# Moving the second batch's front of an attention kernel behind the first score tiles

## Chip, cores, metric

The kernel runs on one core of a Trainium2 chip. The metric is the device time of one execution in microseconds (us). Before the change three runs gave 232.41, 233.00 and 233.81 us, a median of 233.0 us.

## What is computed

Two batches of 512 tokens with 128 features pass through four parts: a gated layer whose weights are picked per batch (`argmax` of `cond_8`), attention with 16 heads whose scores are mixed by a convolution over neighbouring heads, and a routed feed-forward layer of 8 experts that is fed by a base matrix plus low-rank (LoRA) parts.

```python
up = jnp.einsum('bsd,bhd->bsh', x, wu) + bu[:, None, :]
gate = jnp.einsum('bsd,bhd->bsh', x, wg) + bg[:, None, :]
out = jnp.einsum('bsh,bdh->bsd', jax.nn.silu(up) * gate, wd) + bd[:, None, :]
...
Q, K, V = query @ Wq.T + bq, query @ Wk.T + bk, query @ Wv.T + bv
scores = einsum('bhqd,bhkd->bhqk', Q, K) / sqrt(8)
scores = conv over the head axis, 3 taps (scores, conv_w) + conv_b
out = softmax(scores) @ V @ Wo.T + bo;  x = x + out
...
out = x @ W_base.T + b_base + lora(x, cond_8, As, Bs) * 2
gates = softmax(out @ wg); each token goes to its best of 8 experts, 128 places each
x = x + gate * expert(out)
```

## The kernel before, in words

Everything is written by hand for five engines, each with its own list of instructions in order, and semaphores between them. PE is the matrix engine (TensorE), DVE the VectorE, ACT the ScalarE, POOL the GpSimd, SP issues the large DMAs. An instruction that waits holds up everything behind it on its engine.

**The head.** PE first does the gated layer of a batch in transposed form: four matmuls of 128x512 (`first_layer(b, i)`, line 896), whose first two ACT turns into `Ub` and `Tb` (lines 380, 382) and DVE into `Sb_` (`smooth`, line 577) and `Hb` (`hidden_front`, line 582). `gated(b)` (line 904) is two more matmuls, which ACT brings to SBUF as `yT` (`y`, line 387). From `yT` come the keys (`project_keys`, line 910; ACT writes them to `Kp` in `keys`, line 392), the queries (`project_queries`, line 914; DVE adds bias and scale in `queries`, line 598) and the values (`project_values`, line 918; DVE line 609). These products are full float32, two passes of the array each.

The queries and the keys of each head go on as a high and a low part. `Qh` is an ACT copy (`high_queries`, line 397), `Ql` the rest (`low_queries`, line 603). The head convolution is folded into the keys: for head `hd`, `kc` is a sum of three scaled and shifted rows of `Kp`. For head 0 DVE does all of it (`first_head`, lines 617, 621, 624). For later heads POOL does the two outer taps (`outer_taps`: `ta` line 277, `tc_` line 279, their sum `td` line 284) and DVE the middle tap (`middle_tap`, line 572). ACT copies `kc` to the high part `Kh` (`high_first`, line 401; `high_half`, line 419), and `Kl` is the rest, by DVE for heads 0 and 1 (lines 630, 789) and by POOL after that (`low_half`, line 272).

A small branch prepares the routed layer: `L928` forms the low-rank product, DVE adds the base matrix (`weffT`, line 592, semaphore `wte`), `L937` multiplies by the gate's weights, ACT stores it (line 406, semaphore `lae`), `L943` multiplies by the output projection, and ACT stores `wz` (line 413, semaphore `wze`).

**The score tiles.** A tile is 128 queries by 512 keys of one head: three matmuls into one of four PSUM banks `SC` (lines 955 to 957), a DVE pass that adds the convolution's bias and finds the row's extreme (`maximum`, line 639), an ACT exponential (`exp`, line 424), a transposition by PE and ACT (lines 1107 and 469) or by DVE and DMA (line 778 and the copies by way of `swap`), and the product with the values (lines 973 to 980). `unit(b, g, u)` is one step of this pipeline; the score tile runs AHEAD = 4 steps in front. There are 256 such steps. The first four score tiles (lines 1130 to 1132) come ahead of the loop, and between them and the loop PE does `project_queries(1)`, `project_values(1)` and three small transpositions (lines 1138 to 1140) that set counters. The second batch's queries and values are taken off PSUM by DVE in the steps 6 to 9 of the loop.

**The order in the head.** PE: both first layers, L928, `gated(0)`, keys 0, queries 0, L937, `gated(1)`, values 0, keys 1, L943, then the first four score tiles. PE's `first_layer(1, 3)` waits for `wte`, since it overwrites the bank that L928 used, and POOL's first `outer_taps` starts when `Kp` of batch 0 is there.

The steps of the loop and the end of the kernel (routing, experts, the write back) are not touched.

Of the kernel before, what the change touches and what calls it, by code (L numbers as in the profile page):

```python
# [19 lines left out]
B, S, C = 2, 512, 128  # L20
# [40 lines left out]
def build(nc, cond, wexp, xT, wqkvo, lora, cols, b2row, w1, w2, consts, xtok, borow, out, swap):  # L61
# [4 lines left out]
    with ExitStack() as ctx:  # L66
# [3 lines left out]
        def sem(name):  # L70
# [49 lines left out]
        spare = sb("spare", [128, 4])  # L120
        nbias = sb("nbias", [128, RING])
# [53 lines left out]
            dump shr pay hot tok six eog add""".split()  # L175
# [76 lines left out]
        def _(pool):  # L252
# [35 lines left out]
            pool.wait_ge(s["ones"], 1)  # L288
            pool.wait_ge(s["wte"], 1)
            pool.tensor_scalar(bbr, ones[:, :], col[:, BB:BB + 1], 1.0, ALU.mult, ALU.mult).then_inc(s["bbb"], 1)  # L290
            pool.wait_ge(s["cw"], 1)
            pool.wait_ge(s["kev"], 1)
            outer_taps(1, 0, 1)
# [5 lines left out]
            outer_taps(3, 0, 1)  # L299
            pool.wait_ge(s["kev"], 2)  # L300
# [64 lines left out]
        def _(act):  # L365
# [33 lines left out]
            def high_first(hd):  # L399
# [5 lines left out]
            act.wait_ge(s["lam"], 1)  # L405
            act.activation(weff[:, :, 0:E], SC[3][:, 0:B * E].rearrange("p (b e) -> p b e", b=B), ACT.Copy)\
                .then_inc(s["lae"], 1)
            high_queries(0)
            y(1)
            high_first(0)  # L410
            keys(1)
            act.wait_ge(s["wzm"], 1)
            act.activation(wz[:, :, :].rearrange("p b m -> p (b m)"), PV[:, 0:B * W], ACT.Copy).then_inc(s["wze"], 1)
            high_first(1)
# [63 lines left out]
            for k in range(AHEAD):  # L478
                exp(k, k)
# [57 lines left out]
        def _(dve):  # L537
# [15 lines left out]
            for b in range(B):  # L553

                dve.tensor_scalar(bs[:, b, :], lo_w[:, 1, :], col[:, LW + b:LW + b + 1], 2.0,
                                  ALU.mult, ALU.mult).then_inc(s["bsc"], 1)
            for b in range(B):
# [31 lines left out]
            for i in range(2):  # L589
                smooth(1, i)  # L590
            dve.wait_ge(s["wtm"], 1)
            dve.tensor_tensor(weffT, MISC[:, B * C:2 * B * C].rearrange("p (b c) -> p b c", b=B),
                              lo_w[:, 3:4, :].broadcast_to([128, B, C]), ALU.add).then_inc(s["wte"], 1)
# [19 lines left out]
            def first_head():  # L613
# [4 lines left out]
                hidden_front(1, 1)  # L618
                queries(0)
# [10 lines left out]
            dve.tensor_tensor(Kl[:, 0, :], kc[:, 0, :], Kh[:, 0, :].bitcast(f32), ALU.subtract).then_inc(s["kl0"], 1)  # L630
            middle_tap(1, 0, 1, 1)
            values(0)
# [152 lines left out]
            for k in range(AHEAD):  # L785
                maximum(k, k, 0)
                if k == 1:
# [85 lines left out]
        def _(pe):  # L873
# [12 lines left out]
            def first_layer(b, i):  # L886
# [6 lines left out]
                elif b and i == 3:  # L893
                    pe.wait_ge(s["wte"], 1)
# [423 lines left out]
```

## Time and profile before

| what | value |
|---|---|
| median of three runs | 233.0 us |
| profiled execution, its own time | 232.46 us |
| span of its trace | 230.6 us |
| busy share of PE, DVE, ACT, POOL | 95%, 82%, 71%, 72% |
| granted clock of PE, mean | 0.995 |
| first score tile begins, loop begins on PE | 22.74 us, 27.57 us |

The trace shows one execution. Times are counted from the start of the span; what lies around the span is 232.46 - 230.6 = 1.86 us. A line of the timeline gives start, duration, engine, source line, operation, the tile written and the tiles read, and in brackets how long the engine stood idle before it and what released it. A float32 product shows as two records (`x2`) for each 128x512 matmul, since it is done in two passes. Matmuls overlap their neighbours, so starts tell more than ends.

### The profile page before, as it was taken

To read this page: it belongs to the slowest core of one execution; us is meant where nothing else is said; L and a number is where in the kernel's file an instruction comes from. 1 tells how busy PE (TensorE), PEld (TensorE's weight loads), DVE (VectorE), ACT (ScalarE), POOL (GpSimd) and SP (SyncE) were. 2 spreads that over 40 slices of the span, in tenths; PEclk is the share of its full clock that TensorE was granted. 3 is DMA by queue.
4 is the path that set the end of the run, shared out by engine and by line. 5 is a ranking of instruction groups with operands and counts; after the bars stand their busy time and mean duration, and the time that the engine had idled before them with its cause. 6 is when DMAs were issued, how large, how long until landed. Compare 5 with 4: busy or idle time off the path is not lost.

```text
span 230.6 us, 5463 instructions
## 1 busy us (share of the span) xinstructions
PE 219.9 (95%) x1741; PEld 178.8 (78%) x1741; DVE 189.7 (82%) x484; ACT 164.2 (71%) x296; POOL 166.2 (72%) x193
## 2 busy tenths in 40 slices
PE   8999998799999999999999999999999999999990
PEld 8445786487888788888878887888788898989980
DVE  2469999989898998999799799979979777793460
ACT  2455598899698988889798898989898681205310
POOL 1019988799979989898988889898982704361785
PEclk9999999999999999999999999999999999999997
DMA  6993004537727463565556365474546540930233
GB/s 207 349 440 120 3 1 153 121 141 169 209 83 204 154 136 139 134 208 132 154 191 136 144 138 189 102 220 150 134 167 139 187 89 21 347 91 3 23 34 34
DMA packets 16117, 33.42 MB, mean 145 GB/s; under 512 B 1618, under 2 KB 12882, under 8 KB 15826
## 3 DMA queue, kind: packets, MB, share of 16 engines
q1 hardware_dynamic: 14514, 31.94, 46.6%
q0 software_dynamic: 1152, 0.52, 2.6%
q10 hardware_dynamic: 432, 0.71, 0.9%
q8 instruction: 11, 0.18, 0.4%
q14 instruction: 8, 0.07, 0.1%
HBM read 20.32 MB, written 13.37 MB: 146 GB/s over the span
## 4 chain that ended last, share of the span: by engine, by line
PE 85%; DVE 5%; DMA 4%; issue 2%; POOLq 1%; POOL 1%; ACT 1%; SPq 1%; DVEq 0%
PE tp L1107 13%; PE sc L955 13%; PE sc L957 11%; PE sc L956 11%; PE pvbank L975 6%; PE pvbank L973 5%; PE tp L1241 3%; PE sc L1219 3%; PE sc L877 2%; PE misc L1002 2%; DMA PT<-swap 2%; DMA swap<-w2s 2%; PE sc L1168 2%; PE sc L1171 2%; PE sc L896 2%
## 5 line engine op out<-in xcount | busy, mean ns | idle before, releaser
L424 ACT ACTIVATE Pb<-Pb,nbias 128x512 f32<-128x512 f32 x128 | 90.2, 719 | 20.0 <-DVE Pb L639 18.6
L639 DVE TENSOR_SCALAR_CACHE_REDUCE Pb<-sc,col 128x512 f32<-128x512 f32 x128 | 91.5, 732 | 10.6 <-PE sc L957 10.4
L955 PE MATMUL sc<-Kh,Ql 128*128 128x512 f32 x124 | 56.5, 456 | 2.1 <-POOL Kl L272 1.3
L957 PE MATMUL sc<-Kh,Qh 128*128 128x512 f32 x124 | 48.9, 395 | 0.0
L956 PE MATMUL sc<-Kl,Qh 128*128 128x512 f32 x124 | 48.7, 393 | 0.0
L1107 PEld LDWEIGHTS tp<-cst,Pb 128*128 128x128 f32 x316 | 38.9, 140 | 11.6 <-ACT PT L469 1.4
L1107 PE MATMUL tp<-cst,Pb 128*128 128x128 f32 x316 | 47.4, 272 | 0.2 <-ACT PT L469 0.2
L469 ACT ACTIVATE PT<-tp 128x512 f32<-128x512 f32 x77 | 44.8, 581 | 1.0 <-PE tp L1107 0.5
L284 POOL TENSOR_TENSOR td<-ta,tc_ 128x512 f32<-128x512 f32 x31 | 43.1, 1390 | 2.6
L272 POOL TENSOR_TENSOR Kl<-kc,Kh 128x512 fp32r<-128x512 f32 x28 | 36.1, 1289 | 10.2 <-ACT Kh L419 9.0
L778 DVE STREAM_TRANSPOSE w2s<-Pb 128x512 f32<-128x512 f32 x45 | 31.6, 703 | 0.0
L279 POOL TENSOR_SCALAR tc_<-Kp,cwS 128x512 f32<-128x512 f32 x31 | 31.6, 1018 | 0.0
L955 PEld LDWEIGHTS sc<-Kh,Ql 128*128 128x128 f32 x124 | 23.4, 189 | 8.1 <-issue 5.4
L973 PE MATMUL pvbank<-PT,Vst 128*32 128x256 f32 x240 | 29.3, 386 | 0.0
L980 PE MATMUL pvbank<-PT,Vst 128*32 128x128 f32 x240 | 29.0, 274 | 0.0
L975 PE MATMUL pvbank<-PT,Vst 128*32 128x256 f32 x120 | 28.7, 382 | 0.3 <-DMA PT<-swap 0.3
L957 PEld LDWEIGHTS sc<-Kh,Qh 128*128 128x128 f32 x124 | 23.3, 188 | 5.5
L572 DVE SCALAR_TENSOR_TENSOR kc<-Kp,col,td 128x512 f32<-128x512 f32 x31 | 27.3, 881 | 0.0
L980 PEld LDWEIGHTS pvbank<-PT,Vst 128*32 128x32 f32 x240 | 25.0, 110 | 0.0
L956 PEld LDWEIGHTS sc<-Kl,Qh 128*128 128x128 f32 x124 | 23.6, 190 | 1.6
L277 POOL TENSOR_SCALAR ta<-Kp,cwS 128x512 f32<-128x512 f32 x31 | 22.0, 710 | 1.9 <-ACT Kp L392 1.7
L359 POOL DMA_INDIRECT out<-PT,to_row x8 | 12.6, 1572 | 8.9 <-issue 7.5
(230 smaller groups left out, 297.9 us busy)
## 6 DMA issues: line engine op xcount, KB each, us to landing
swap<-w2s SPq DMA_DIRECT2D x15, 768.0 KB, 3.3
PT<-swap SPq DMA_DIRECT2D x60, 192.0 KB, 3.8
w1s<-in_w SPq DMA_DIRECT2D x1, 2048.0 KB, 9.6
w2s<-in_w SPq DMA_DIRECT2D x1, 2048.0 KB, 7.8
cst<-in_consts SPq DMA_DIRECT2D x1, 652.0 KB, 5.1
xTs<-in_xT SPq DMA_DIRECT2D x2, 256.0 KB, 3.1
we<-in_wexp SPq DMA_DIRECT2D x2, 256.0 KB, 3.4
b2s<-in_b2row SPq DMA_DIRECT2D x1, 512.0 KB, 10.4
```

Of the source, the lines that this page charges most:

```text
L272: pool.tensor_tensor(Kl[:, n, :], kc[:, n, :], Kh[:, n, :].bitcast(f32), ALU.subtract)\
L284: pool.tensor_tensor(td[:, n, :], ta[:, :], tc_[:, :], ALU.add).then_inc(s["d"], 1)
L424: act.activation(Pb[:, k, :], Pb[:, k, :], ACT.Exp, bias=nbias[:, k:k + 1], scale=-1.0)\
L469: act.activation(dst, bank[:, :].rearrange("p (k q) -> p k q", k=QT), ACT.Copy)\
L639: dve.tensor_scalar(Pb[:, k, :], SC[k % 4][:, :], cb, None, ALU.subtract, ALU.min, accum_out=nbias[:, k:k + 1]).then_inc(s["mx"], 1)
L955: pe.matmul(SC[k][:, :], ql, Kh[:, h2, :], start=True, stop=False)
L956: pe.matmul(SC[k][:, :], qh, Kl[:, h2, :], start=False, stop=False)
L957: pe.matmul(SC[k][:, :], qh, Kh[:, h2, :], start=False, stop=True).then_inc(s["sc"], 1)
L973: mm = pe.matmul(bank, v, PTA[:, 2 * w + i, k, :], **ends)
L975: pe.matmul(bank, v, PTB[:, w, :, k, 0:64].rearrange("p i (t c) -> p t i c", t=2), **ends)
L980: pe.matmul(bank[:, 128 * t:128 * t + 128], Vst[:, kk, 2 * w + i, :], x, start=(kk == 0), stop=(kk == QT - 1))
L1107: mm = pe.transpose(bank[:, k * 128:(k + 1) * 128], Pb[:, u % RING, k * 128:(k + 1) * 128], ident)
```

## The change

The numbers in the order listings below are line numbers of each kernel's own file.

- **Queries of batch 0.** The bias and scale move from DVE to ACT, with a pre-scaled bias `bqs` that DVE makes in one 128x1 instruction at the start. PE projects them right behind the keys.
- **DVE's chain for the keys of head 0** no longer has `hidden_front(1, 1)` and the queries between its first and second instruction. `hidden_front(1, 1)` comes behind `Kl` of head 0.
- **POOL's first outer taps** wait until `kc` of head 0 is finished, and the small `bbr` instruction (line 290) goes behind the third set of taps.
- **The small branch and the rest of batch 1** move: L928 behind values 0, into another bank; `gated(1)` behind the first score tile; keys 1, L937, values 1, L943 and queries 1 between the fourth score tile and the loop. ACT's and DVE's parts move with them; `values(0)` on DVE goes behind the first `maximum`.

The diff, without the lines that only add the name of a semaphore:

```diff
@@ -285,11 +286,9 @@
             fetch_taps(1, 1, 1)
-            pool.wait_ge(s["ones"], 1)
-            pool.wait_ge(s["wte"], 1)
-            pool.tensor_scalar(bbr, ones[:, :], col[:, BB:BB + 1], 1.0, ALU.mult, ALU.mult).then_inc(s["bbb"], 1)
             pool.wait_ge(s["cw"], 1)
             pool.wait_ge(s["kev"], 1)
+            pool.wait_ge(s["kc"], 1)
             outer_taps(1, 0, 1)
@@ -297,6 +296,9 @@
             outer_taps(3, 0, 1)
+            pool.wait_ge(s["ones"], 1)
+            pool.wait_ge(s["wte"], 1)
+            pool.tensor_scalar(bbr, ones[:, :], col[:, BB:BB + 1], 1.0, ALU.mult, ALU.mult).then_inc(s["bbb"], 1)
             pool.wait_ge(s["kev"], 2)
@@ -402,16 +404,13 @@
             keys(0)
-            act.wait_ge(s["lam"], 1)
-            act.activation(weff[:, :, 0:E], SC[3][:, 0:B * E].rearrange("p (b e) -> p b e", b=B), ACT.Copy)\
-                .then_inc(s["lae"], 1)
+            act.wait_ge(s["qmm"], 1)
+            act.wait_ge(s["bqs"], 1)
+            act.activation(q32[0][:, :], FRONT[0][2][:, :], ACT.Identity, bias=bqs[:, 0:1], scale=-float(DH) ** -0.5)\
+                .then_inc(s["qev"], 1)
+            act.wait_ge(s["qev"], 1)
             high_queries(0)
-            y(1)
             high_first(0)
-            keys(1)
-            act.wait_ge(s["wzm"], 1)
-            act.activation(wz[:, :, :].rearrange("p b m -> p (b m)"), PV[:, 0:B * W], ACT.Copy).then_inc(s["wze"], 1)
-            high_first(1)
@@ -475,8 +474,18 @@
-            for k in range(AHEAD):
-                exp(k, k)
+            exp(0, 0)
+            high_first(1)
+            y(1)
+            exp(1, 1)
+            exp(2, 2)
+            keys(1)
+            act.wait_ge(s["lam"], 1)
+            act.activation(weff[:, :, 0:E], PV[:, 0:B * E].rearrange("p (b e) -> p b e", b=B), ACT.Copy)\
+                .then_inc(s["lae"], 1)
+            exp(3, 3)
+            act.wait_ge(s["wzm"], 1)
+            act.activation(wz[:, :, :].rearrange("p b m -> p (b m)"), PV[:, 0:B * W], ACT.Copy).then_inc(s["wze"], 1)
             high_half(2, 0)
@@ -554,6 +563,7 @@
                                   ALU.mult, ALU.mult).then_inc(s["bsc"], 1)
+            dve.tensor_scalar(bqs[:, :], col[:, BQ:BQ + 1], -float(DH) ** -0.5, None, ALU.mult).then_inc(s["bqs"], 1)
             for b in range(B):
@@ -588,9 +598,6 @@
                 smooth(1, i)
-            dve.wait_ge(s["wtm"], 1)
-            dve.tensor_tensor(weffT, MISC[:, B * C:2 * B * C].rearrange("p (b c) -> p b c", b=B),
-                              lo_w[:, 3:4, :].broadcast_to([128, B, C]), ALU.add).then_inc(s["wte"], 1)
             hidden_front(1, 0)
@@ -615,8 +622,6 @@
                 dve.tensor_scalar(kw[:, :], Kp[:, 0, 0:S], col[:, CW:CW + 1], None, ALU.mult).then_inc(s["k0"], 1)
-                hidden_front(1, 1)
-                queries(0)
                 dve.wait_ge(s["k0"], 1)
@@ -628,8 +633,11 @@
             dve.tensor_tensor(Kl[:, 0, :], kc[:, 0, :], Kh[:, 0, :].bitcast(f32), ALU.subtract).then_inc(s["kl0"], 1)
+            hidden_front(1, 1)
+            dve.wait_ge(s["wtm"], 1)
+            dve.tensor_tensor(weffT, PV[:, B * C:2 * B * C].rearrange("p (b c) -> p b c", b=B),
+                              lo_w[:, 3:4, :].broadcast_to([128, B, C]), ALU.add).then_inc(s["wte"], 1)
             middle_tap(1, 0, 1, 1)
-            values(0)
@@ -784,6 +792,8 @@
                 maximum(k, k, 0)
+                if k == 0:
+                    values(0)
                 if k == 1:
@@ -891,7 +901,7 @@
                 elif b and i == 3:
-                    pe.wait_ge(s["wte"], 1)
+                    pe.wait_ge(s["wefe"], B)
                 at = (WU, WGT)[i // 2] + i % 2 * 128
@@ -923,25 +933,17 @@
             first_layer(1, 1)
-            pe.wait_ge(s["wefe"], B)
-            for b in range(B):
-                mm = pe.matmul(MISC[:, (B + b) * C:(B + b + 1) * C], bs[:, b, :], lo_w[:, 0, :], start=True, stop=True)
-            mm.then_inc(s["wtm"], 1)
             gated(0)
...
             project_keys(0)
+            project_queries(0)
             first_layer(1, 3)
-            project_queries(0)
+            project_values(0)
+            pe.wait_ge(s["hm"], 3)
             for b in range(B):
-                mm = pe.matmul(SC[3][:, b * E:(b + 1) * E], weffT[:, b, :], col[:, WG:WG + E], start=True, stop=True)
-            mm.then_inc(s["lam"], 1)
-            gated(1)
-            pe.wait_ge(s["lae"], 1)
-            project_values(0)
-            project_keys(1)
-            pe.matmul(PV[:, 0:B * W], wq[:, 4, :], weff[:, :, :].rearrange("p b m -> p (b m)"), start=True, stop=True)\
-                .then_inc(s["wzm"], 1)
+                mm = pe.matmul(PV[:, (B + b) * C:(B + b + 1) * C], bs[:, b, :], lo_w[:, 0, :], start=True, stop=True)
+            mm.then_inc(s["wtm"], 1)
@@ -1130,9 +1132,19 @@
                 pe.matmul(SC[k][:, :], qh, Kh[:, 0, :], start=False, stop=True).then_inc(s["sc"], 1)
+                if k == 0:
+                    gated(1)
+            project_keys(1)
+            pe.wait_ge(s["wte"], 1)
+            for b in range(B):
+                mm = pe.matmul(PV[:, b * E:(b + 1) * E], weffT[:, b, :], col[:, WG:WG + E], start=True, stop=True)
+            mm.then_inc(s["lam"], 1)
+            project_values(1)
+            pe.wait_ge(s["lae"], 1)
+            pe.matmul(PV[:, 0:B * W], wq[:, 4, :], weff[:, :, :].rearrange("p b m -> p (b m)"), start=True, stop=True)\
+                .then_inc(s["wzm"], 1)
             pe.wait_ge(s["wze"], 1)
             project_queries(1)
-            project_values(1)
             pe.wait_ge(s["cst"], 16)
```

**PE, from the fourth score tile to the counters ahead of the loop.** `sc` is a score bank, `tp`, `misc` and `pvbank` are other PSUM banks, `O` holds `weffT`, `col` the gate's weights. Before:

```order
L1130 MATMUL sc<-Kh,Ql 128x512 [waits s_vev]
L1131 MATMUL sc<-Kl,Qh 128x512
L1132 MATMUL sc<-Kh,Qh 128x512
L914 MATMUL pvbank<-yT,wq 128x512 [waits s_hm,s_wze]
L918 MATMUL misc<-wq,yT 128x128 x4
L1138 MATMUL tp<-cst,ones 128x128 [waits s_cst]
```

Now:

```order
L1132 MATMUL sc<-Kh,Ql 128x512 [waits s_vev]
L1133 MATMUL sc<-Kl,Qh 128x512
L1134 MATMUL sc<-Kh,Qh 128x512
L920 MATMUL tp<-yT,wq 128x512 [waits s_yev]
L1140 MATMUL pvbank<-col,O 128x8 [waits s_wte]
L1140 MATMUL pvbank<-col,O 128x8
L928 MATMUL misc<-wq,yT 128x128 x4
L1144 MATMUL pvbank<-weff,wq 128x272 [waits s_lae]
L924 MATMUL pvbank<-yT,wq 128x512 [waits s_hm,s_wze]
L1150 MATMUL tp<-cst,ones 128x128 [waits s_cst]
```

The keys of batch 1 (L920), the two small products of the branch (L1140, L1144) and the values of batch 1 (L928) have come in, each with a wait on ACT or DVE of its own; the queries of batch 1 (L924) are now last, still behind `wze`.

**ACT, from the end of keys 0 to the second head group's `Kh`.** `RAW` holds the queries of batch 0 in float32, `PT` and `Pb` are work tiles. Before:

```order
L406 ACTIVATE weff<-sc 128x2x8 [waits s_lam]
L397 ACTIVATE Qh<-RAW 128x512 [waits s_qev]
L387 ACTIVATE yT<-tp,we 128x512 [waits s_ymm]
L401 ACTIVATE Kh<-kc 128x512 [waits s_kc]
L392 ACTIVATE Kp<-tp,col 128x512 [waits s_kmm]
L413 ACTIVATE wz<-pvbank 128x272 [waits s_wzm]
L401 ACTIVATE Kh<-kc 128x512 [waits s_kc]
L424 ACTIVATE Pb<-Pb,nbias 128x512 [waits s_mx] x4
L419 ACTIVATE Kh<-kc 128x512 [waits s_sc,s_kc]
```

Now:

```order
L409 ACTIVATE RAW<-sc,bqs 128x512 [waits s_bqs,s_qmm]
L399 ACTIVATE Qh<-RAW 128x512 [waits s_qev]
L403 ACTIVATE Kh<-kc 128x512 [waits s_kc]
L423 ACTIVATE Pb<-Pb,nbias 128x512 [waits s_mx]
L403 ACTIVATE Kh<-kc 128x512 [waits s_kc]
L389 ACTIVATE yT<-tp,we 128x512 [waits s_ymm]
L423 ACTIVATE Pb<-Pb,nbias 128x512 [waits s_mx] x2
L394 ACTIVATE Kp<-tp,col 128x512 [waits s_kmm]
L484 ACTIVATE weff<-pvbank 128x2x8 [waits s_lam]
L423 ACTIVATE Pb<-Pb,nbias 128x512 [waits s_mx]
L488 ACTIVATE wz<-pvbank 128x272 [waits s_wzm]
L418 ACTIVATE Kh<-kc 128x512 [waits s_sc,s_kc]
```

The four exponentials, which stood in one piece behind everything else, now have `Kh` of head 1, `yT` of batch 1, `Kp` of batch 1 and the two copies of the branch between and behind them; the branch's last copy (`wz`) stands behind the fourth exponential.

## Rows read from the trace of the kernel before

**Rows 1.** Stretches: length, busy us (instructions) of PE, PEld, DVE, ACT, POOL; PEclk, DMA, GB/s.

```profile
21.00:27.50 6.50, 6.00 (x28) 4.19 (x27) 6.41 (x12) 3.91 (x7) 6.13 (x7) 1.00 0.00 0
27.50:36.00 8.50, 8.10 (x47) 6.56 (x46) 8.50 (x20) 7.76 (x14) 7.18 (x9) 1.00 0.01 3
36.00:46.00 10.00, 8.23 (x40) 5.67 (x40) 10.00 (x22) 8.46 (x17) 7.87 (x10) 1.00 0.56 158
...
61.00:220.00 159.00, 158.84 (x1386) 133.89 (x1385) 137.08 (x360) 120.44 (x218) 118.77 (x134) 1.00 0.51 142
```

**Rows 2.** Timeline, PE: start, duration, engine, line, operation, tiles, idle before.

```profile
11.70 0.61 PE L928 MATMUL misc<-lo_w,bs 128*128 128x128 f32 x4
12.15 1.88 PE L904 MATMUL sc<-PT,we 128*128 128x512 f32 x4
...
14.90 1.10 PE L910 MATMUL sc<-yT,wq 128*128 128x512 f32 x2
...
17.55 0.51 PE L937 MATMUL sc<-col,O 128*128 128x8 f32 x4
...
19.71 1.05 PE L918 MATMUL sc<-wq,yT 128*128 128x128 f32 x8
...
21.62 0.62 PE L943 MATMUL pvbank<-weff,wq 128*128 128x272 f32 x2
22.74 0.47 PE L1130 MATMUL sc<-Kh,Ql 128*128 128x512 f32 x1 [0.50 <-DVE Kl L630]
...
27.57 0.48 PE L955 MATMUL sc<-Kh,Ql 128*128 128x512 f32 x1
```

**Rows 3.** Timeline, DVE, the head and the first step of the loop.

```profile
14.17 0.42 DVE L592 TENSOR_TENSOR O<-misc,lo_w 128x256 f32<-128x256 f32 x1
15.01 0.75 DVE L582 SCALAR_TENSOR_TENSOR PT<-pvbank,we,PT 128x512 f32<-128x512 f32 x1 [0.42 <-PE pvbank L896]
16.75 0.48 DVE L617 TENSOR_SCALAR Pb<-Kp,col 128x512 f32<-128x512 f32 x1 [1.00 <-ACT Kp L392]
...
18.48 0.74 DVE L621 SCALAR_TENSOR_TENSOR Pb<-Kp,col,Pb 128x512 f32<-128x512 f32 x1
19.25 1.64 DVE L624 SCALAR_TENSOR_TENSOR kc<-Kp,col,Pb 128x512 f32<-128x512 f32 x1
20.81 0.68 DVE L603 TENSOR_TENSOR Ql<-RAW,Qh 128x512 fp32r<-128x512 f32 x1
21.59 1.00 DVE L630 TENSOR_TENSOR Kl<-kc,Kh 128x512 fp32r<-128x512 f32 x1
...
24.21 0.73 DVE L639 TENSOR_SCALAR_CACHE_REDUCE Pb<-sc,col 128x512 f32<-128x512 f32 x1
...
25.55 0.89 DVE L789 TENSOR_TENSOR Kl<-kc,Kh 128x512 fp32r<-128x512 f32 x1
...
28.84 0.74 DVE L639 TENSOR_SCALAR_CACHE_REDUCE Pb<-sc,col 128x512 f32<-128x512 f32 x1
```

**Rows 4.** Timeline, ACT, the head.

```profile
16.03 0.69 ACT L392 ACTIVATE Kp<-sc,col 128x512 f32<-128x512 f32 x1 [1.28 <-PE sc L910]
...
20.93 0.63 ACT L401 ACTIVATE Kh<-kc 128x512 fp32r<-128x512 f32 x1 [0.33 <-DVE kc L624]
...
22.40 0.39 ACT L413 ACTIVATE wz<-pvbank 128x272 f32<-128x272 f32 x1
...
24.99 1.39 ACT L424 ACTIVATE Pb<-Pb,nbias 128x512 f32<-128x512 f32 x2 [0.63 <-DVE Pb L639]
```

**Rows 5.** Timeline, POOL, the first outer taps.

```profile
16.89 0.91 POOL L277 TENSOR_SCALAR ta<-Kp,cwS 128x512 f32<-128x512 f32 x1 [1.74 <-ACT Kp L392]
...
18.55 1.80 POOL L284 TENSOR_TENSOR td<-ta,tc_ 128x512 f32<-128x512 f32 x1
```

**Rows 6.** Lines 572 and 284, all instances: duration ns min/median/max, first and last start.

```profile
L572 DVE SCALAR_TENSOR_TENSOR kc<-Kp,col,td x31: 743/795/1217, 22.5 to 175.1; 128x512 f32<-128x512 f32 x31
L284 POOL TENSOR_TENSOR td<-ta,tc_ x31: 1282/1296/1797, 18.5 to 171.2; 128x512 f32<-128x512 f32 x31
```

More of the change, by code:

```diff
@@ L120, in build @@
         spare = sb("spare", [128, 4])
+        bqs = sb("bqs", [128, 1])
         nbias = sb("nbias", [128, RING])
@@ L174, in build @@
             slt gm wtm wte lam lae wzm wze bbb xbo xtk xto disp0 disp1 dsp dtea dted onr k0 kl0 b2g hm0 hmm heva hevd hevx eom
-            dump shr pay hot tok six eog add""".split()
+            dump shr pay hot tok six eog add bqs""".split()
         s = {n: sem("s_" + n) for n in names}
```

## The prediction

> **What bounds the kernel now.** I read the busy time by stretch first, since one share for the whole span says nothing of the head. From 61 us on PE works 158.84 of 159 us: what reaches that point late ends late, and nothing is caught up there [rows 1]. From 27.5 to 46 us another engine sets the pace: DVE is busy 8.50 of 8.50 and 10.00 of 10.00 us, while PE has 0.40 and 1.77 us free, all at the full granted clock [rows 1]. So there are two moments to watch. One is when PE begins its loop, 27.57 us [rows 2]. The other is when DVE takes the loop's first tile, 28.84 us [rows 3]: a delay there goes through to the end, a delay of PE alone may vanish in its 2.17 us.
>
> Then the timeline of the head, engine by engine. The first score tile starts at 22.74, released by DVE's `Kl` (21.59, 1.00 us long) [rows 2, 3]. The chain above it runs over `Kp` on ACT (16.03) [rows 4], then DVE's 617, 621 and 624 at 16.75, 18.48 and 19.25 [rows 3]. Two things stretch it. Two other DVE instructions stand between 617 and 621, and 624 takes 1.64 us beside POOL's `td`, where the same kind (621) takes 0.74 [rows 3, 5].
>
> **The sum, in order of time.** A queued instruction on DVE or ACT starts 0.06 to 0.1 us before its predecessor ends; the times below include that.
>
> 1. *L928 leaves its place.* It held PE from 11.70 to 12.15 [rows 2], so `gated(0)`, `yT`, keys 0 and `Kp` come 0.44 earlier: keys at 14.46, `Kp` done at 15.59 + 0.69 = 16.28 [rows 2, 4].
> 2. *Queries on ACT.* PE projects them from about 15.4 to 16.4. ACT has nothing else then; with 0.69 for a 128x512 eviction and 0.63 for the high part [rows 4], `Qh` is there at 17.8. `kc` is not ready by then, so both are hidden. The extra `bqs` on DVE lies in its idle time ahead of the first layer: nothing.
> 3. *DVE's chain.* 617 from 16.31 (0.48), 621 to 17.56 (0.74) [rows 3]. 624 now has no POOL instruction beside it: 0.74 in place of 1.64, done at 18.33 in place of 20.89. Before, 1.85 us went from there to the first tile (20.89 to 22.74 [rows 2, 3]); `Ql`, `Kh`, `Kl` and POOL's first tap stand to each other as before, so the first tile starts at 20.2. That is **2.5 us early**.
> 4. *What PE must still do.* Before, 22.74 to 27.57, 4.83 us, held the four tiles, queries 1, values 1 and the counters [rows 2]. Now `gated(1)`, keys 1, L937 and L943 come in as well: 1.72, 0.86, 0.44 and 0.50 us (1.88, 1.10, 0.51 and 0.62 long, less the overlap with the next) [rows 2]. With no wait at all the loop starts at 20.2 + 4.83 + 3.52 = 28.55. Even so PE is **1.0 us later than before**: between values 0 and the first tile it now stands idle for 1.7 us, from about 18.5.
> 5. *POOL starts late.* Its first `ta` waits for `kc`, 18.4 instead of 16.89. The first three instructions took 3.46 us (16.89 to 20.35) [rows 5]; without any hindrance about 2.6 (`td` is never under 1.28 [rows 6]). I take 3.46, since `Ql` and `Kl` lie beside them: done at 21.9, bounds 21.0 and 22.3. `middle_tap(1)` waits for it. DVE fills the time with `hidden_front(1, 1)` and `weffT` (0.75, 0.42 [rows 3]), then idles. Middle tap 0.80 (0.74 to 1.22 [rows 6]), then the first maximum 0.73 [rows 3]: 23.4. Before, the first maximum ended at 24.94. Of the 2.5 us only 1.5 are left.
> 6. *The chain through ACT.* Here the products that moved are paid for. Exp 0 to 24.1, `Kh(1)` to 24.7, `yT(1)` to 25.3 (0.70, 0.63, and 0.69 as for `Kp` [rows 4]). PE's last tile is issued by 24.85 and keys 1 can start at 25.45: 0.6 idle, plus 0.1 where the fourth tile waits for `values(0)`. Exp 1 ends at 25.9. Exp 2 needs maximum 2, and that stands on DVE behind `Kl(1)`, which starts at 24.7.
> 7. *Size of `Kl(1)`.* Its own row says 0.89 [rows 3]. But it now meets POOL's second `td`, which begins near 24.4 and ends near 25.7. The row nearest to that is 624: started 0.70 after a `td`, ended 0.54 after that `td`'s end [rows 3, 5]. So I take 1.45 (bounds 0.68 and 1.64). `Kl(1)` is done at 26.15, maximum 2 at 26.85, exp 2 at 27.55, `Kp(1)` at 28.2, the branch's small copy at 28.3, exp 3 at 29.0. With 0.89 all of this from exp 2 on is 0.55 earlier.
> 8. *Back to PE.* L943 waits for the small copy: 28.4, 0.75 idle. ACT copies `wz` after exp 3: 29.4 (0.39 [rows 4]). Queries 1 wait for that: 29.5. With 0.86 for them and 0.25 for the counters the loop starts at **30.6**, 3.0 later than 27.57. As a check, 28.55 plus the idle pieces 0.1, 0.6, 0.75 and 0.6 is 30.6.
> 9. *DVE* finds the loop's first tile at 31.55 instead of 28.84: **+2.7 us**. PE's 3.0 matters less than this, since PE has idle time until 46 us. POOL's first `Kl` ends about 31.4 and is needed at 34.4, so `bbr`, now in front of it, is hidden; without that cover it would cost its 0.4. The steps of the loop itself are the same instructions as before. PE's free pieces in the head (at most 1.7 us) are of the size of those between 36 and 46, where the granted clock stayed 1.00 [rows 1]: nothing for the clock.
>
> Against the profiled execution (232.46 us) this is 235.2. Against the median of the runs (233.0, 0.5 above it) it is **235.7 us**.
>
> On step 7 the Trainium skill (SBUF, "Who interferes with whom") says that a DVE instruction with two SBUF inputs and a GpSimd one that reads SBUF exclude each other, and whoever starts first holds the shared ports for its whole length. By it the row 0.89 would not apply, and the loop would start at 30.6, not at 30.05; the trace agrees in the pair 624 and `td`.
>
> **Rivals.**
> - *ACT's chain doesn't hold PE.* If PE finds everything ready, it starts the loop at 28.55, DVE at 29.5, +0.65: **233.7 us**. For it: each idle piece is under 1 us and hangs on a few tenths. Against: exp 0 cannot come before POOL's `td`, and seven ACT instructions of 0.6 to 0.7 us follow one another.
> - *Faster.* DVE gives back time between 27.5 and 46 us. There its two-source instructions are lengthened by POOL, line 572 up to 1.217 against 0.743 us [rows 6], four such come to about 1.6 us. If POOL, shifted against DVE, misses them all, and PE has the case above with a `Kl(0)` of 0.68 instead of 1.00 (0.3 earlier), it is +0.65 - 0.3 - 1.6 = -1.25: **231.7 us**. It decides from where PE's waits between first tile and loop come to under 0.3 us. Against: both shift by nearly the same amount, 2.3 to 2.7. The Trainium skill (Perfetto Trace Analysis, "Optimization Strategy") counts interleaving stretches with different busiest engines as a way to gain; here the busiest engine of the next stretch is DVE, and it is not given work earlier.
> - *More collisions.* The same lever the other way: four or five two-source instructions of the loop's start that ran free (795 ns is the median [rows 6]) now meet a `td`, 0.3 to 0.4 us each, +1.5: **237.2 us**.
> - *The change doesn't do what it says.* 624 stays long for a reason other than POOL: `kc` and all behind it 0.9 later, **236.6 us**.
>
> **How the numbers follow.** Forecast 0.70, with a range of its own of 234.6 to 236.7 (`td`, the middle tap and `Kl(1)` at their bounds). ACT's chain doesn't hold 0.13, faster 0.06, more collisions 0.08, not what it says 0.03. A measurement of this kernel can tell about 0.5% (1.2 us) from no change. Slower by more than that: 0.70 + 0.08 + 0.03 = 0.81. Within it: 0.13 (233.7). Faster: 0.06. The range 233.4 to 237.1 takes in the second case and half of the collisions, and leaves out the faster case and the rest.
>
> **What would show it.** Right: first score tile near 20.2; 624 at 0.74; POOL's first `td` ending near 21.9 with DVE idle before the middle tap; PE idle ahead of keys 1, L943 and queries 1; PE's loop near 30.6 and DVE's first tile there near 31.5; the same rhythm later on, shifted. Wrong: a loop start before 29 on PE, or DVE's run up to 46 us shorter by more than 1 us.

## The result and the profile after

| | before | changed |
|---|---|---|
| runs, median (lowest to highest), us | 233.41 (232.41 to 234.62), 6 runs | 235.75 (235.36 to 236.50), 6 runs |
| profiled execution, us | 232.46, span 230.6 | 236.50, span 234.7 |
| ratio, 95% interval | | 1.0108 [1.0071, 1.0146] |
| granted clock, whole span | | 0.996 |

The changed kernel is slower by about 2.5 us (1.7 to 3.4). The forecast was 235.7 us. The profiled execution of the changed kernel is the slowest of its six runs and that of before nearly the fastest of its own, so the two spans differ by 4.1 us. I first read what the head (all that lies ahead of the loop) does to the time, and then come to the rest of the 4.1 us.

One correction first. The part on the kernel before says that there are 256 steps; there are 128 steps and 128 score tiles, 4 of which come ahead of the loop. Tiles are counted below from the first of the 128, so that the loop's first tile is the 5th. No number of the prediction used this.

Times of the two traces need one shift. The head of this execution ran 0.27 us earlier, from the first layer on (6.21 against 6.48 us, where the input arrives). Where a time is compared with the prediction I add 0.27 and give it in brackets.

PE's timeline of the changed kernel (start, duration, engine, line, operation, tiles, count, idle before and what ended it). It answers to [rows 2].

```profile
14.19 1.10 PE L920 MATMUL sc<-yT,wq 128*128 128x512 f32 x2
...
19.96 0.47 PE L1132 MATMUL sc<-Kh,Ql 128*128 128x512 f32 x1 [1.61 <-DVE Kl L635]
20.73 1.88 PE L914 MATMUL tp<-PT,we 128*128 128x512 f32 x4
...
23.84 0.50 PE L1132 MATMUL sc<-Kh,Ql 128*128 128x512 f32 x1
...
25.09 1.13 PE L920 MATMUL tp<-yT,wq 128*128 128x512 f32 x2 [0.28 <-ACT yT L389]
...
26.42 1.14 PE L928 MATMUL misc<-wq,yT 128*128 128x128 f32 x8
27.79 0.72 PE L1144 MATMUL pvbank<-weff,wq 128*128 128x272 f32 x2 [0.23 <-ACT weff L484]
29.00 1.13 PE L924 MATMUL pvbank<-yT,wq 128*128 128x512 f32 x2 [0.49 <-ACT wz L488]
...
30.21 0.48 PE L957 MATMUL sc<-Kh,Ql 128*128 128x512 f32 x1
```

The first score tile is at 19.96 (20.23) instead of 22.74: 2.5 us earlier. The loop is at 30.21 (30.48) instead of 27.57: 2.9 us later. In between lie the work that was moved in and three waits. Every wait is released by ACT. The idle times in brackets are smaller than what is lost, because the modelled end of a group covers a part of the gap. I measure by starts instead. In the kernel before, the values of batch 1 and the instruction behind them are:

```profile
26.43 1.05 PE L918 MATMUL misc<-wq,yT 128*128 128x128 f32 x8
27.32 0.27 PE L1138 MATMUL tp<-cst,ones 128*128 128x128 f32 x1
```

From start to start that is 0.89. In the changed kernel values 1 starts at 26.42, so L1144 could have started at 27.31; it started at 27.79, and 0.48 is lost. In the same way keys 1 lose 0.56 (the fourth tile starts at 23.84, and on PE before it is 0.69 from one tile to the next, 23.51 to 24.20), and queries 1 lose 0.71 (27.79 and the 0.50 of step 4).

DVE's timeline, same kernel; it answers to [rows 3].

```profile
17.36 0.75 DVE L629 SCALAR_TENSOR_TENSOR kc<-Kp,col,Pb 128x512 f32<-128x512 f32 x1
...
21.75 0.76 DVE L582 SCALAR_TENSOR_TENSOR kc<-Kp,col,td 128x512 f32<-128x512 f32 x1 [0.95 <-POOL td L285]
22.44 0.74 DVE L647 TENSOR_SCALAR_CACHE_REDUCE Pb<-sc,col 128x512 f32<-128x512 f32 x1
...
24.50 1.16 DVE L799 TENSOR_TENSOR Kl<-kc,Kh 128x512 fp32r<-128x512 f32 x1
...
31.20 0.75 DVE L647 TENSOR_SCALAR_CACHE_REDUCE Pb<-sc,col 128x512 f32<-128x512 f32 x1 [3.49 <-PE sc L959]
```

The instruction that took 1.64 us beside POOL's `td` takes 0.75. DVE then waits 0.95 for that same `td`, which now comes later. Ahead of the loop's first tile DVE idles 3.49 us; it takes that tile at 31.20 (31.47), 2.6 us later than before.

ACT and POOL, same kernel; they answer to [rows 4] and [rows 5].

```profile
16.96 0.63 ACT L399 ACTIVATE Qh<-RAW 128x512 fp32r<-128x512 f32 x1
...
24.37 0.67 ACT L389 ACTIVATE yT<-tp,we 128x512 f32<-128x512 f32 x1
...
26.36 0.72 ACT L423 ACTIVATE Pb<-Pb,nbias 128x512 f32<-128x512 f32 x1 [0.72 <-DVE Pb L647]
27.00 0.67 ACT L394 ACTIVATE Kp<-tp,col 128x512 f32<-128x512 f32 x1
27.57 0.17 ACT L484 ACTIVATE weff<-pvbank 128x16 f32<-128x16 f32 x1
27.63 0.72 ACT L423 ACTIVATE Pb<-Pb,nbias 128x512 f32<-128x512 f32 x1
28.55 0.40 ACT L488 ACTIVATE wz<-pvbank 128x272 f32<-128x272 f32 x1 [0.20 <-PE pvbank L1144]
```

```profile
18.32 0.95 POOL L278 TENSOR_SCALAR ta<-Kp,cwS 128x512 f32<-128x512 f32 x1 [15.26 <-DVE kc L629]
...
20.45 1.27 POOL L285 TENSOR_TENSOR td<-ta,tc_ 128x512 f32<-128x512 f32 x1
...
23.83 1.28 POOL L285 TENSOR_TENSOR td<-ta,tc_ 128x512 f32<-128x512 f32 x1
```

Exp 2 on ACT (the third exponential, 26.36) waits 0.72 for DVE's maximum; `Kp(1)` and the branch's small copy stand behind it, and PE's L1144 behind them. Exp 3 stands ahead of the copy `wz`, and queries 1 behind that. This is the chain that holds PE.

By stretches (busy us and instructions of PE, PEld, DVE, ACT, POOL; granted clock; DMA share; GB/s), the answer to [rows 1]:

```profile
27.50:30.50 3.00, 2.28 (x9) 1.25 (x9) 0.20 (x1) 1.76 (x5) 2.70 (x4) 1.00 0.00 0
30.50:39.00 8.50, 8.50 (x48) 7.04 (x47) 7.80 (x18) 6.46 (x11) 5.54 (x8) 1.00 0.06 25
39.00:49.00 10.00, 8.26 (x46) 5.48 (x49) 10.00 (x24) 8.97 (x18) 8.11 (x9) 1.00 0.53 141
...
64.00:223.00 159.00, 157.73 (x1371) 132.08 (x1370) 136.58 (x354) 119.87 (x217) 117.01 (x132) 1.00 0.50 140
```

DVE has 0.20 us of work in the 3 us ahead of the loop. In the loop's first 8.5 us PE is now the engine without a gap and DVE has 0.70 free, the other way round from before [rows 1]. From 39 us on DVE is full again. So a little comes back here: DVE is late by 2.4 us at the 5th tile, the loop's first, and by 2.0 at the 13th (without the 0.27).

**The rest of the 4.1 us in this pair of traces.** The delay of DVE's tiles is 1.7 to 2.0 us from the 13th to the 25th tile, jumps to 3.3 by the 33rd, stays there to the 101st, and is 4.1 at the 128th. The same kernel shows the first jump in one execution and not in another. SyncE's queue writes the transposed exponentials (they lie in the memory that is named `w2s`) to DRAM and reads them back; I call this an exchange. Below are its second write, the read behind it, and the 25th and 33rd tile of DVE, for the changed kernel in this execution:

```profile
48.71 0.34 SPq L229 DMA_DIRECT2D swap<-w2s  x1
53.59 1.73 SPq L234 DMA_DIRECT2D PT<-swap  x4
```

```profile
56.40 0.70 DVE L647 TENSOR_SCALAR_CACHE_REDUCE Pb<-sc,col 128x512 f32<-128x512 f32 x1
...
68.92 0.70 DVE L647 TENSOR_SCALAR_CACHE_REDUCE Pb<-sc,col 128x512 f32<-128x512 f32 x1
```

and for the same kernel in another execution (e8 below):

```profile
49.51 0.34 SPq L229 DMA_DIRECT2D swap<-w2s  x1
54.24 1.73 SPq L234 DMA_DIRECT2D PT<-swap  x4
```

```profile
57.23 0.70 DVE L647 TENSOR_SCALAR_CACHE_REDUCE Pb<-sc,col 128x512 f32<-128x512 f32 x1
...
68.49 0.71 DVE L647 TENSOR_SCALAR_CACHE_REDUCE Pb<-sc,col 128x512 f32<-128x512 f32 x1
```

From write to read it is 4.88 us in the first and 4.73 in the second; between the two tiles 12.52 and 11.26 us (before: 4.22 and 11.20). The change alone therefore doesn't bring the 1.3 us; I leave them out of its account. PE is free for 1.27 us between 64 and 223 us here (157.73 busy above), for 0.16 in before's last stretch [rows 1] and for 0.46 in e8 between 64 and 223. The 0.8 us at the end are not explained; from the 101st tile to the 128th the same kernel took 0.4 us less in e8. The trace of e5 below has the jump of 1.3 us as well and a span 1.1 us above that of before, while its median is that of before. That would fit if the slower executions of before had the jump too, but none of them was traced.

### The profile page after: what moved, and what is told of

Read it like the earlier page. It is cut to its first block, busy times and chain, and to the rows that moved or that the text cites. A ratio compares the mean times of both kernels' runs of the same rounds, so it can differ in the third digit from the quotient of the medians.

```text
span 234.7 us, 5466 instructions
## 1 busy us (share of the span) xinstructions
PE 220.6 (94%) x1741; PEld 177.7 (76%) x1741; DVE 188.8 (80%) x484; ACT 164.3 (70%) x297; POOL 164.7 (70%) x193
## 4 chain that ended last, share of the span: by engine, by line
PE 75%; DVE 8%; ACT 6%; issue 5%; POOL 2%; DMA 2%; POOLq 1%; SPq 0%; DVEq 0%; ACTq 0%
PE tp L1109 12%; PE sc L957 11%; PE sc L959 10%; PE sc L958 9%; PE pvbank L977 6%; PE pvbank L975 6%; DVE Pb L647 4%; PE tp L1253 3%; PE sc L1231 3%; ACT Pb L423 2%; PE misc L1004 2%; PE sc L1180 2%; PE sc L1183 2%; PE sc L906 2%; ACT PT L468 1%
## 5 line engine op out<-in xcount | busy, mean ns | idle before, releaser
L285 POOL TENSOR_TENSOR td<-ta,tc_ 128x512 f32<-128x512 f32 x31 | 41.9, 1352 | 2.6
L957 PEld LDWEIGHTS sc<-Kh,Ql 128*128 128x128 f32 x124 | 23.4, 189 | 7.4 <-issue 4.9
```

The source lines that it names most:

```text
L285: pool.tensor_tensor(td[:, n, :], ta[:, :], tc_[:, :], ALU.add).then_inc(s["d"], 1)
L957: pe.matmul(SC[k][:, :], ql, Kh[:, h2, :], start=True, stop=False)
```

## The experiments

"Head shift" is the loop's start on PE minus the start of keys 0, less the 12.67 us that before has (14.90 to 27.57). Where L928 no longer stands ahead of keys 0, 0.44 is taken off as well. It removes the different arrival of the input in each execution. "DVE shift" is the same for the first tile of the loop on DVE (before 14.90 to 28.84, 13.94). Ratios are against the kernel before in runs on the same chip.

| kernel | head shift, us | DVE shift, us | ratio [95%] |
|---|---|---|---|
| changed | +2.91 | +2.6 | 1.0108 [1.0071, 1.0146] |
| e1, without POOL's wait | +4.82 | +4.5 | 1.0216 [1.0158, 1.0273] |
| e2, queries ahead of the branch | +2.15 | +1.9 | 1.0089 [1.0056, 1.0122] |
| e3, DVE's part alone | -0.36 | 0.0 | 0.9999 [0.9965, 1.0033] |
| e4, before + 1.72 us on PE | +1.73 | +1.4 | 1.0103 [1.0071, 1.0136] |
| e5, gaps filled | -0.19 | -0.5 | 0.9999 [0.9974, 1.0024] |
| e6, ACT's order | +1.86 | +1.6 | 1.0089 [1.0055, 1.0124] |
| e7, e1 with PE kept busy | +3.41 | +3.1 | 1.0127 [1.0086, 1.0168] |
| e8, changed kernel again | +2.91 | +2.6 | 1.0119 [1.0085, 1.0153] |
| e9, e5 with `bbr` early | -0.18 | -0.5 | 0.9995 [0.9969, 1.002] |

e1 to e4 ran together on one chip, e5 to e8 on another, e9 on a third. The head shift of the changed kernel comes out the same in two executions.

### e1: POOL's wait for `kc` taken out of the changed kernel

```diff
             pool.wait_ge(s["kev"], 1)
-            pool.wait_ge(s["kc"], 1)
             outer_taps(1, 0, 1)
```

> The changed kernel, but POOL's first outer taps start as soon as Kp is there, as they did before the change, and no longer wait for kc of head 0. My theory (the late loop comes from the chain through ACT and PE's queue; POOL's wait only trades one delay for another): the last instruction for kc of head 0 grows from 0.75 back to about 1.6 us beside POOL's td, the first score tile comes 0.9 us later (near 20.9), the middle tap starts at about the same time as now (21.7), the loop starts on PE within 0.5 us of the changed kernel's 30.2, and the total is 0 to 0.5 us above the changed kernel. Rival (POOL's wait is what makes the change slower): the first exponential and all behind it come 0.8 to 1.0 us sooner, the total falls by as much.

Both expectations were far too low. By the ratios, each against before on its own chip, e1 is 2.3 to 2.5 us above the changed kernel (1.0216 against 1.0119 in e8 and 1.0108). PE and then DVE of e1:

```profile
21.59 0.47 PE L1131 MATMUL sc<-Kh,Ql 128*128 128x512 f32 x1 [2.81 <-DVE Kl L634]
22.36 3.15 PE L913 MATMUL tp<-PT,we 128*128 128x512 f32 x4
```

```profile
17.00 1.06 DVE L625 SCALAR_TENSOR_TENSOR Pb<-Kp,col,Pb 128x512 f32<-128x512 f32 x1
18.10 1.06 DVE L628 SCALAR_TENSOR_TENSOR kc<-Kp,col,Pb 128x512 f32<-128x512 f32 x1
19.09 1.75 DVE L609 TENSOR_TENSOR Ql<-RAW,Qh 128x512 fp32r<-128x512 f32 x1
```

The collisions are back: 1.06 and 1.06 for 0.75 each, beside POOL's one-input `ta` (16.63 to 17.53) and `tc_` (17.52 to 18.63), and `Ql` 1.75 for 0.68, beside `td` (18.71 to 20.29). Against keys 0 (14.62 here) the first tile starts 1.2 us later than in the changed kernel, yet the loop 1.9 later. The rest comes from something else. `gated(1)`, the same four matmuls, takes 3.15 us instead of 1.88. The stretches show why (columns as above; the granted clock is the third number from the end):

```profile
22.00:23.00 1.00, 1.00 (x5) 0.67 (x4) 1.00 (x3) 0.00 (x0) 0.92 (x3) 0.91 0.00 0
23.00:26.00 3.00, 3.00 (x5) 1.36 (x5) 1.48 (x4) 1.69 (x3) 2.83 (x4) 0.50 0.07 22
26.00:27.00 1.00, 1.00 (x5) 0.78 (x5) 0.36 (x1) 0.23 (x1) 0.92 (x2) 0.88 0.00 0
```

The granted clock is 0.50 (1.2 instead of 2.4 GHz) from 23 to 26 us, after PE had stood idle for 2.81 us and had begun to work again at 21.59. In the changed kernel the wait at the same place is 1.61 us and the clock stays 1.00.

### e7: e1 with PE kept busy in that wait

```diff
+            keep_busy(SC[0], 8)
             pe.wait_ge(s["qhi"], 1)
```

(on top of e1; the matmuls write a bank that the first tile then overwrites)

> e1_no_kc_wait with eight products of ones on a free bank put into PE's idle time before the first score tile (1.8 us of its 2.8). In e1 the granted clock fell to 0.50 from 22.9 to 26.2 us, behind that idle time. Theory (the idle time made it fall, and the fall cost the 1.5 to 2 us by which e1 exceeds my expectation): the granted clock stays 1.00, PE's loop starts near 30.9 instead of 32.5, the total falls by 1.3 to 2 us against e1, to 0 to 0.7 us above the changed kernel. Rival (the clock fell for another reason, or its fall is taken in later): the total stays within 0.5 us of e1's, 2.1% above the kernel before.

```profile
20.95 0.47 PE L1132 MATMUL sc<-Kh,Ql 128*128 128x512 f32 x1 [1.03 <-DVE Kl L634]
21.71 1.88 PE L913 MATMUL tp<-PT,we 128*128 128x512 f32 x4
```

```profile
23.00:25.00 2.00, 2.00 (x9) 1.51 (x8) 1.52 (x6) 1.73 (x3) 1.84 (x4) 1.00 0.07 18
```

The clock stays at 1.00 and `gated(1)` is back at 1.88. The head shift falls from 4.82 to 3.41, and the whole kernel by about 2.1 us going by the two ratios, whose intervals just overlap. The first tile is as late against keys 0 as in e1 (6.97 us). So of e1's additional 1.9 us in the head 1.4 were the clock and 0.5 the collisions. The expectation for the clock held. Here one edit fills the gap and keeps the clock, and nothing else changes; this shows that the idle time made it fall.

### e3: the kernel before, with the chain on DVE shortened and nothing moved to behind the tiles

Added to before: the queries of batch 0 on ACT and POOL's wait for `kc`. PE's order is that of before.

```diff
+            pool.wait_ge(s["kc"], 1)
             outer_taps(1, 0, 1)
...
             keys(0)
+            act.activation(q32[0][:, :], FRONT[0][2][:, :], ACT.Identity, bias=bqs[:, 0:1], scale=-float(DH) ** -0.5)\
+                .then_inc(s["qev"], 1)
+            high_queries(0)
...
-                queries(0)
                 dve.wait_ge(s["k0"], 1)
```

> The kernel before with three parts of the change alone: queries of batch 0 on ACT, DVE's chain without them, and POOL's first taps behind kc of head 0. PE's order and the place of the second batch's work are those of before. Theory (in the old order PE is packed until 22.2 us, so that an earlier kc finds no free PE): kc is ready 1.3 to 1.6 us earlier, the first score tile only 0.4 to 0.6 us earlier than 22.74, the middle tap later since POOL starts later, and the total is within 0.4 us of the kernel before. Rival (these parts are a gain of their own, and only PE's new order spoils it): the total is more than 1 us below the kernel before.

DVE, then PE:

```profile
18.84 0.75 DVE L630 SCALAR_TENSOR_TENSOR kc<-Kp,col,Pb 128x512 f32<-128x512 f32 x1
...
23.25 0.76 DVE L579 SCALAR_TENSOR_TENSOR kc<-Kp,col,td 128x512 f32<-128x512 f32 x1 [1.96 <-POOL td L285]
```

```profile
22.12 0.59 PE L1136 MATMUL sc<-Kh,Ql 128*128 128x512 f32 x1
...
27.45 0.48 PE L961 MATMUL sc<-Kh,Ql 128*128 128x512 f32 x1
```

Keys 0 start at 15.14 here against 14.90, so 0.24 comes off. `kc` is done at 19.35 instead of 20.89, 1.5 us earlier, and the first tile starts at 21.9 instead of 22.74, 0.9 earlier (0.4 to 0.6 were expected). Of this the loop's start on PE keeps 0.36, DVE's first tile there nothing, and the total nothing that the interval (0.8 us either way) would show. DVE's middle tap waits 1.96 us for POOL, which started late. This is the half of the change that makes the chain faster, and it is worth nothing by itself: PE has its own work ahead of the loop, and the early `kc` is followed by a late `td`. `values(0)` stands behind the middle tap on DVE and ends at 24.61, and PE's fourth tile, which waits for it, starts at 24.66, 0.96 behind the third where 0.69 is the free distance.

### e4: the kernel before with two more matmuls between its first tiles and the loop

```diff
             pe.wait_ge(s["wze"], 1)
+            for _ in range(2):
+                pe.matmul(FRONT[1][2][:, :], wq[:, 0, :], yT[:, 1, :], start=True, stop=True)
             project_queries(1)
```

The two matmuls (four records) repeat work whose result is overwritten.

> The kernel before, with the second batch's query product done three times instead of once (same result, 1.72 us more of PE work between the fourth score tile and the loop). Theory (DVE stands at the loop's entry waiting for PE, and then has no idle moment, so a late loop start goes through to the end in full): PE's loop starts 1.7 us later and the total grows by 1.5 to 1.8 us. Rival (PE's idle time between 36 and 46 us takes it in): the total grows by less than 0.5 us.

```profile
25.23 1.88 PE L1135 MATMUL pvbank<-yT,wq 128*128 128x512 f32 x4
...
28.95 0.47 PE L955 MATMUL sc<-Kh,Ql 128*128 128x512 f32 x1
```

They add 1.72 us to PE; the loop starts 1.73 later, DVE's first tile 1.42, and the whole is 1.0103 [1.0071, 1.0136], +2.4 us (1.7 to 3.2). The rival, that the later slack of PE absorbs it, falls. Nothing of a delay ahead of the loop is given back. The total is above the 1.5 to 1.8 us that were expected, though the interval takes these in; why it is above the 1.4 to 1.7 us of the head isn't shown. Its trace also has the long second exchange (5.02 us from write to read) and the jump of 1.3 us.

### e2 and e6: the waits on ACT, taken away one at a time

e2 lets PE do queries 1 ahead of the branch's `wz` product, which goes to another bank, and waits for `wz` only in the loop (ACT's copy reads the other bank, and the counters' transpositions go to a third):

```diff
             pe.wait_ge(s["lae"], 1)
-            pe.matmul(PV[:, 0:B * W], wq[:, 4, :], weff[:, :, :].rearrange("p b m -> p (b m)"), start=True, stop=True)\
-                .then_inc(s["wzm"], 1)
-            pe.wait_ge(s["wze"], 1)
             project_queries(1)
+            pe.matmul(TP[0][:, 0:B * W], wq[:, 4, :], weff[:, :, :].rearrange("p b m -> p (b m)"), start=True, stop=True)\
+                .then_inc(s["wzm"], 1)
...
             for u in range(TURN):
+                if u == 1:
+                    pe.wait_ge(s["wze"], 1)
                 unit(0, 0, u)
```

> The changed kernel, but PE projects the second batch's queries before the branch's last product, which goes to another bank, and the loop no longer waits for ACT's copy wz (only the second step's transposition does). Theory (PE's loop start sets the time, and the wait for wz through ACT's queue is a part of it): PE's loop starts near 29.1 instead of 30.2, DVE takes the loop's first tile near 30.1 instead of 31.2, and the total is 1.0 to 1.2 us below the changed kernel. Rival (the loop is held by DVE's or POOL's chain, or the head's delay is taken in later): the total stays within 0.3 us of the changed kernel.

```profile
28.20 1.12 PE L924 MATMUL pvbank<-yT,wq 128*128 128x512 f32 x2 [0.23 <-ACT weff L484]
```

The head shift falls by 0.76 where 1.1 was expected. That is the 0.71 that queries 1 lost by waiting for `wz`, and little else: they still stand behind the wait for the small copy. In the total the interval does not part it from the changed kernel.

e6 changes ACT's order alone:

```diff
+            y(1)
             exp(0, 0)
             high_first(1)
-            y(1)
             exp(1, 1)
-            exp(2, 2)
             keys(1)
...
-            exp(3, 3)
+            exp(2, 2)
             act.wait_ge(s["wzm"], 1)
...
+            exp(3, 3)
```

> The changed kernel with ACT's queue alone put in another order: yT of batch 1 before the first exponential, Kp and the small copy before the third, wz before the fourth. Theory (the order on ACT makes PE wait): PE's loop starts near 29.3 instead of 30.2, the total is 0.5 to 1.2 us below the changed kernel run beside it. Rival (the waits on ACT only hide a shortage elsewhere): within 0.3 us of the changed kernel.

```profile
28.21 1.13 PE L924 MATMUL pvbank<-yT,wq 128*128 128x512 f32 x2 [0.49 <-ACT wz L487]
```

The head shift falls by 1.05, to +1.86. The place where ACT's copies stand among the exponentials is thus worth 1 us on PE, as expected. The total, 1.0089, is 0.7 us below e8, with intervals that overlap; that it is faster is likely and not shown.

### e5: the moved work put into PE's gaps

On top of e6's idea: `gated(1)` goes into the wait ahead of the first tile, keys 1 and the branch's small product behind tile 0, the `wz` product behind tile 2; ACT does `y(1)`, `keys(1)` and the small copy ahead of the first exponential; DVE does `hidden_front(1, 1)` between its two `kc` instructions and `values(0)` ahead of the middle tap.

```diff
             mm.then_inc(s["wtm"], 1)
+            gated(1)
...
                 if k == 0:
-                    gated(1)
-            project_keys(1)
-            pe.wait_ge(s["wte"], 1)
+                    project_keys(1)
+                    pe.wait_ge(s["wte"], 1)
...
+                elif k == 2:
+                    pe.wait_ge(s["lae"], 1)
+                    pe.matmul(PV[:, 0:B * W], wq[:, 4, :], weff[:, :, :].rearrange("p b m -> p (b m)"), start=True, stop=True)\
+                        .then_inc(s["wzm"], 1)
             project_values(1)
```

> The changed kernel with PE's idle time in the head filled: hidden_front(1,1) goes ahead of the last tap of head 0, gated(1) comes before the first score tile, ACT takes yT, Kp and the two copies of the branch before the exponentials that stand behind them, keys 1 and the branch's products go between the tiles, values(0) on DVE goes into its wait for POOL. Theory (the change lost its 2.5 us because PE stood idle before and between the first tiles and ACT's queue let it wait): first tile near 20.6 (0.6 later than in the changed kernel), PE's loop start near 27.1 to 27.4, DVE's first tile of the loop near 28.3, total 0 to 0.6 us below the kernel before, that is over 2 us below the changed kernel. Rival (the early score tiles themselves or POOL's late taps cost the time): the total stays at least 1 us above the kernel before.

```profile
18.49 1.88 PE L913 MATMUL tp<-PT,we 128*128 128x512 f32 x4
20.80 0.47 PE L1132 MATMUL sc<-Kh,Ql 128*128 128x512 f32 x1 [0.43 <-DVE Kl L636]
...
27.42 0.48 PE L957 MATMUL sc<-Kh,Ql 128*128 128x512 f32 x1
```

The first tile is later than in the changed kernel by 0.5 us (keys 0 start at 14.50 here), and the loop starts 3.1 us earlier. The loss is gone: 0.9999 [0.9974, 1.0024], at the edge of the 0 to 0.6 us below before that were expected. The loop's start is 0.2 ahead of before and DVE's first tile there 0.5, and the total isn't, so no version here beats both. The lead on DVE is gone four tiles later: the middle tap at 31.02 takes 1.30 beside POOL's `Kl` (30.49 to 31.77), where the one at this place before took 0.78.

### e9: e5 with POOL's `bbr` ahead of its wait

```diff
             pool.wait_ge(s["kev"], 1)
+            pool.wait_ge(s["ones"], 1)
+            pool.wait_ge(s["bsc"], B)
+            pool.tensor_scalar(bbr, ones[:, :], col[:, BB:BB + 1], 1.0, ALU.mult, ALU.mult).then_inc(s["bbb"], 1)
             pool.wait_ge(s["kc"], 1)
```

> e5_filled with one more edit: POOL makes bbr (0.37 us) while it waits for kc of head 0 instead of behind the third taps, where it stands ahead of the first Kl that POOL makes for the loop. Theory (in e5 that Kl ended at 31.77 with PE waiting for it from 31.2, and DVE lost 0.5 us there): POOL's first Kl is ready 0.3 to 0.4 us earlier, DVE's ninth tile comes 0.2 to 0.4 us earlier than in e5, the total is 0.2 to 0.6 us below the kernel before, at the edge of what five rounds can tell. Rival (DVE's blocked middle tap sets this place, not POOL's Kl): no difference from e5.

No difference from e5, as the rival had it: POOL's first `Kl` starts only 0.12 us earlier against keys 0 (30.16 against 30.49 in e5, whose keys start 0.21 later), and the middle tap that follows on DVE (30.82) is still held beside it (1.18 us, 1.30 in e5, 0.74 when free). That `bbr` costs nothing where it stands, as step 9 has it, is borne out within the interval.

## Why the prediction was right, and where it was off

- **The result.** 235.7 us forecast, 235.75 measured, and +2.7 forecast against +2.5 by the ratio. The agreement of the medians to 0.05 us is luck; the runs of one kernel spread over more than 1 us.
- **Steps 1 to 3**, the earlier tile, held to 0.1 us: keys 0 at 14.46 (14.46 forecast), `Qh` done at 17.86 (17.8), `kc` at 18.38 (18.33), first tile at 20.23 (20.2), with the 0.27 added. The Trainium skill (SBUF — State Buffer, "Who interferes with whom") has a two-input DVE instruction and a GpSimd one that reads SBUF exclude each other. The trace agrees: 1.64 us beside `td`, 0.75 without, and 1.75 for `Ql` in e1. The case also shows that POOL's wait doesn't save the time of the collision but moves it to another place, as POOL's lateness.
- **Step 4**, the size of the work that moved in, was the core of the forecast. From first tile to loop it is 10.25 us (19.96 to 30.21), and 8.50 less the three waits; 8.35 were forecast without waits (20.2 to 28.55) and 10.4 with them. e4 shows by itself that such work is paid in full, and e3 that the early tile brings nothing measurable in return.
- **Step 5** held: `td` done at 21.99 (21.9), middle tap 0.76 (0.80), first maximum done at 23.4 (23.4).
- **Step 6**: keys 1 at 25.36 (25.45). e6 shows that the order of ACT causes 1.05 us of the loop's lateness.
- **Step 7 is the term that was mis-sized.** `Kl(1)` took 1.16 us; I took 1.45, and its own row said 0.89 [rows 3]. That it would be held by the `td` beside it was right, and so was the size taken from the row of 624, which ended 0.54 after its `td`: `Kl(1)` ended at 25.66, 0.55 after `td` (23.83 to 25.11). The row of 0.89 was that of a held instruction too, beside `ta` (25.20 to 25.89 in before); free, it takes 0.69 (e1, 27.32). What was off is where that `td` stands, from 24.10 to 25.38 with the 0.27 added and not from 24.4 to 25.7. The 0.3 us too much passes to exp 2, `Kp(1)` and the small copy, and is most of what parts step 8's first time from the measured one; at the loop 0.1 of it is left.
- **Step 8**: the `wz` product (L943, now L1144) at 28.06 (28.4), queries 1 at 29.27 (29.5), loop at 30.48 (30.6). There are three waits, as forecast: 0.56, 0.48 and 0.71 us lost by starts, 1.75 in all (forecast 0.6, 0.75 and 0.6, 1.95 in all).
- **Step 9**: DVE's first tile at 31.47 (31.55). The text had DVE set the pace from there and PE's lateness vanish. In the changed kernel PE has no gap in its first 8.5 us of loop and DVE has 0.70, so the two changed places for that stretch and some 0.4 us came back. The sentence on the clock came out right on a weak reading: it set a single gap of 1.7 us beside the 1.77 us that PE had free in all between 36 and 46, where the longest single gap was 1.34 us (before 41.28). That 1.61 us would do no harm was thus not known beforehand, and e1 and e7 show how near it was to failing: with 1.2 us more of idle PE, e1's clock cost 1.4 us in the head.
- **The rivals.** "ACT's chain doesn't hold PE" is ruled out by the three waits and by e6. "Faster" fell, since DVE gave back 0.4 and not 1.6 (by its own terms it should have said 231.4 us, since four times the 0.47 between 1.217 and 0.743 is 1.9). "More collisions" fell: DVE's delay did not grow from the 5th tile to the 13th. "Doesn't do what it says" fell with the 0.75.
- **What stays open**: the 1.3 us of some executions around the second exchange through DRAM and the 0.8 us at the end of this trace, which no experiment of mine addressed; the total of e4, some 0.7 to 1 us above its head; and whether the gains of e2 and e6 reach the end.

## What to carry to other kernels

In this kernel, and I would expect it in others that are built like it, an earlier first result is worth nothing if the engine that must be full from then on has only had its work moved to behind it. Add up what that engine still has to do until the steady part begins, then its waits; that sum is the answer, and the instant of the first result is not. Work that is moved goes into a gap that the trace shows (e5), and each copy that it needs goes ahead of the longer instructions on the copying engine (e6). Removing a collision by a wait moves the time to the engine that waits; look at who needs its result next. Before a gap on PE is lengthened, look at the granted clock behind the longest gaps.

## What the runs showed of the hardware that was not expected

- **The clock after a gap.** In e1 PE was idle for 2.81 us and resumed at 21.59; the granted clock was still 1.00 from 22.0 to 22.5, 0.82 from 22.5 to 23, and 0.50 for the whole of 23 to 26 us, so it fell after the work had resumed and not in the gap. With 1.61 us idle (changed kernel), or 1.03 us behind the filling matmuls (e7), it was 1.00 throughout. The fall lengthened a group of four matmuls from 1.88 to 3.15 us.
- **How long a held DVE instruction lasts.** A DVE instruction with two SBUF inputs that started while a POOL instruction was running ended 0.53 to 0.55 us after the end of that POOL instruction: 624 (0.54) and `Kl(1)` (0.55) in before, `Kl(1)` in the changed kernel (0.55), the three in e1 (0.53, 0.53, 0.55), the middle taps above in e5 and e9 (0.55). POOL's `ta` and `tc_`, which read one tile, held it as its `td` did, which reads two.
- **One DRAM transfer of varying length.** From the second exchange's write to its read it took 4.22 us in before, 4.73 and 4.88 in two executions of the changed kernel, and up to 5.42 in e5, while the first, third and fourth took 3.3 us in each of these. Over the eleven traces, DVE's run from its 25th to its 33rd tile was 1.3 us longer than before with 4.88 us and with everything from 5.02 on; with 4.91 (e6) it was 0.3 longer and with up to 4.73 at most 0.1. So the length of the write goes with the jump and doesn't settle it.
